# Which head of a quad ScalarE exponentiates in the second attention, and where in its order it does so

## The reference

```python
q = (hidden_states @ wq.T).reshape(B, S, HEADS, HEAD_DIM).transpose(0, 2, 1, 3)   # 32 heads of 8
k = (hidden_states @ wk.T).reshape(B, S, HEADS, HEAD_DIM).transpose(0, 2, 1, 3)
v = (hidden_states @ wv.T).reshape(B, S, HEADS, HEAD_DIM).transpose(0, 2, 1, 3)
scores = jnp.einsum('bhqd,bhkd->bhqk', q, k) / scale
scores = scores + _rel_bias(rel_pos, S)[None, None]
attn = jax.nn.softmax(scores, axis=-1)
ctx = jnp.einsum('bhqk,bhkd->bhqd', attn, v)
return ctx.transpose(0, 2, 1, 3).reshape(B, S, HIDDEN) @ wo.T
```

## Time and profile before

| | us |
|---|---|
| median of 3 runs | 876.03 |
| lowest and highest | 875.99, 877.25 |
| the profiled execution's own time | 876.34 |
| its span on the core | 874.6 |
| second attention in it (first scores to last mix) | 354 to 670 |
| TensorE matmul busy over the span | 806.8 |
| VectorE, ScalarE, GpSimd busy | 667.3, 579.4, 422.2 |

### The profile page before, as it was taken

The page is one execution under the profiler, slowest core; times in us unless marked ns, Lnnn a source line. Parts: engine busy times, 40 slices in busy tenths (PEclk is TensorE's granted clock), DMA queues, the critical chain, the costliest instruction groups (busy, mean ns, idle before and its releaser), DMA issues.

```text
span 874.6 us, 20901 instructions
## 1 busy us (share of the span) xinstructions
PE 806.8 (92%) x7097; PEld 677.9 (78%) x7097; DVE 667.3 (76%) x2136; ACT 579.4 (66%) x1232; POOL 422.2 (48%) x725
## 2 busy tenths in 40 slices
PE   4876999999999999899999999999998999999994
PEld 3554778888888899667777777777766988999984
DVE  5987889888896555778898888979886463487657
ACT  2777868687787533677878777777766233366646
POOL 0353223233253311576767667676765357355423
PEclk9899999999999999999999999999999899999998
DMA  7111220201001010111010211201013112345444
GB/s 218 35 40 43 80 86 12 87 14 37 26 1 49 25 38 25 43 34 31 22 55 23 63 42 37 66 22 43 23 59 120 37 64 95 92 129 134 128 161 170
DMA packets 55017, 54.86 MB, mean 63 GB/s; under 512 B 18209, under 2 KB 49185, under 8 KB 54914
## 3 DMA queue, kind: packets, MB, share of 16 engines
q1 hardware_dynamic: 51506, 44.18, 17.1%
q0 software_dynamic: 3408, 9.34, 3.1%
HBM read 32.85 MB, written 20.65 MB: 61 GB/s over the span
## 4 chain that ended last, share of the span: by engine, by line
PE 68%; DVE 15%; ACT 9%; issue 6%; POOL 1%; DMA 1%; DVEq 0%; ACTq 0%; SPq 0%; POOLq 0%
PE ps L448 13%; PE ps L449 12%; PE ps L450 12%; PE ps L992 10%; PE ps L1003 5%; PE ps L684 3%; PE ps L731 2%; DVE G L2182 2%; PE ps L771 2%; PE ps L976 2%; DVE wu_rows L2182 2%; ACT G L1596 1%; PE ps L1249 1%; PE ps L753 1%; PE ps L1213 1%
## 5 line engine op out<-in xcount | busy, mean ns | idle before, releaser
L2568 POOL TENSOR_SCALAR_AFFINE_SELECT G<-G 128x256 f32<-128x256 f32 x128 | 75.9, 617 | 150.1 <-ACT G L1422 149.9
L1596 ACT ACTIVATE G<-ps 128x512 f32<-128x512 f32 x184 | 102.7, 602 | 39.9 <-PE ps L992 38.3
L448 PE MATMUL ps<-WU 128*128 128x256 f32 x384 | 116.3, 303 | 11.4 <-DVE WU L1977 6.5
L2616 POOL TENSOR_SCALAR G<-G,small 128x256 f32<-128x256 f32 x214 | 99.8, 483 | 51.6 <-DVE small L2182 49.9
L2182 DVE CUSTOM_DVE_ANT_0 G<-ps,nb 128x256 f32<-128x256 f32 x296 | 108.3, 420 | 10.6 <-PE ps L731 9.4
L449 PE MATMUL ps<-WU 128*128 128x256 f32 x384 | 108.3, 282 | 0.0
L450 PE MATMUL ps<-WU 128*128 128x256 f32 x384 | 108.3, 282 | 0.0
L2616 POOL TENSOR_SCALAR wu_rows<-wu_rows,small 128x256 f32<-128x256 f32 x154 | 71.7, 482 | 38.7 <-DVE small L2182 37.7
L448 PEld LDWEIGHTS ps<-WU 128*128 128x128 f32 x384 | 72.8, 190 | 18.0 <-DVE WU L1977 7.3
L992 PE MATMUL ps<-ident,G 128*128 128x128 f32 x592 | 83.5, 278 | 3.0 <-ACT G L1596 2.9
L2182 DVE CUSTOM_DVE_ANT_0 wu_rows<-ps,nb 128x256 f32<-128x256 f32 x216 | 79.5, 420 | 7.4 <-PE ps L731 6.5
(11 more groups left out here) (267 smaller groups left out, 2356.2 us busy)
## 6 DMA issues: line engine op xcount, KB each, us to landing
xs<-G SPq DMA_DIRECT2D x8, 645.0 KB, 6.6
G<-xs SPq DMA_DIRECT2D x39, 128.0 KB
G<-x SPq DMA_DIRECT2D x17, 256.0 KB, 3.1
G<-in_x SPq DMA_DIRECT2D x16, 256.0 KB, 2.8
wu_rows<-yy SPq DMA_DIRECT2D x8, 512.0 KB, 7.0
x<-G SPq DMA_DIRECT2D x15, 256.0 KB, 2.2
wu_rows<-in_wu SPq DMA_DIRECT2D x8, 384.0 KB, 4.9
wraw<-in_wu SPq DMA_DIRECT2D x16, 128.0 KB, 2.2
```

The lines of the kernel that those rows point to most:

```text
L448: pe.matmul(o, lh, rh, start=start, stop=False, skip_group_check=True)
L1596: act.activation(probT(n), halves(2 + n % 2), ACT.Exp).then_inc(probT_taken, 1)
L2568: m = pool.affine_select(out=u, in_=u, compare_op=ALU.is_ge, fill=0.0, base=0, pattern=[[0, 2], [1, P]], channel_multiplier=-1)
L2616: m = pool.tensor_scalar(p, p, -1.0, mneg[:, k:k + 1], ALU.mult, ALU.add)
```

## The change

In the slots with three heads on GpSimd the first head of the quad, and no longer the last, is ScalarE's. Its exponential stands between the two pairs of takes (behind what already stood between them) and no longer at the slot's end. GpSimd shifts heads 1, 2 and 3 of the quad in the place of 0, 1 and 2. Which semaphore a `turn` waits for and whether a `take` is an Exp or a copy follow the head (`on_pool`). Slots 0 and 4 (two heads each) and slot 3 (none on ScalarE) stay.

```diff
         def shifts(n):
             quad, j = divmod(n, 4)
-            return (sum(POOL_SHIFTS) * (quad // QUADS) + sum(POOL_SHIFTS[:quad % QUADS])
-                    + min(j + 1, POOL_SHIFTS[quad % QUADS]))
+            before = sum(POOL_SHIFTS) * (quad // QUADS) + sum(POOL_SHIFTS[:quad % QUADS])
+            return before + sum(on_pool(4 * quad + k) for k in range(j + 1))
+        def on_pool(n):
+            quad, j = divmod(n, 4)
+            few = POOL_SHIFTS[quad % QUADS]
+            return j > 0 if few == 3 else j < few
 # TensorE, turn(n)
-                    if j < POOL_SHIFTS[quad % QUADS]:
+                    if on_pool(n):
                         pe.wait_ge(prob_shifted, shifts(n))
                     else:
                         pe.wait_ge(prob_ready, n + 1 - shifts(n))
 # ScalarE, take(n)
-                    if n % 4 < POOL_SHIFTS[n // 4 % QUADS]:
+                    if on_pool(n):
                         act.activation(probT(n), halves(2 + n % 2), ACT.Exp).then_inc(probT_taken, 1)
 # ScalarE, one(i, first, left)
                         if q == 5 and left:
                             stage_v(2, i + 1)
                         if q == 7 and left:
                             q_heads(2, i + 1, 1)
+                        if POOL_SHIFTS[q] == 3:
+                            exponential(H2 * i + 4 * q)
                         if before >= 0:
                             take(before + 2)
                             take(before + 3)
...
-                        for j in range(POOL_SHIFTS[q], 4):
-                            exponential(H2 * i + 4 * q + j)
+                        if POOL_SHIFTS[q] == 2:
+                            for j in range(2, 4):
+                                exponential(H2 * i + 4 * q + j)
 # GpSimd
-                    for j in range(POOL_SHIFTS[q]):
-                        shifted(H2 * i + 4 * q + j)
+                    for j in range(4):
+                        if on_pool(4 * q + j):
+                            shifted(H2 * i + 4 * q + j)
```

More of the change, by code:

```diff
@@ L979, in turn @@
                 def turn(n):
-                    quad, j = divmod(n, 4)
                     if n == 0:
                         pe.wait_ge(ffn_step, 3 * iterations[1] - 2)
-                    if j < POOL_SHIFTS[quad % QUADS]:
+                    if on_pool(n):
                         pe.wait_ge(prob_shifted, shifts(n))
```

## The result

| | before | changed |
|---|---|---|
| median of 4 runs, us | 876.64 (875.99 to 878.23) | 882.11 (881.51 to 884.63) |
| profiled execution, us | 876.34 | 882.60 |
| its span, us | 874.6 | 880.5 |
| second attention, first scores to the scores of the last slot, us | 306.94 | 311.86 |

The first three of the four runs before are those of the median 876.03 above. The changed kernel takes 1.0065 times as long, with a 95% interval of 1.0047 to 1.0082. By this ratio it is 5.7 us more, by the two medians 5.5; 4.8 (0.55%) had been predicted.

A forecast was written before the change was run, and what follows sets the result against it. The prediction took waits at handovers between engines, not any engine's amount of work, to bound the kernel. Its terms, 3.15 + 2.0 - 0.33 = +4.8 us on the median of 876.03, gave 880.8 us (879.5 to 882; wide 877.6 to 884.0).

The forecast's parts named there:

- What bounds the kernel: Whole kernel: no engine's amount of work is at stake; what counts is which engine waits for another at each handover.
- rival A: Second attention: TensorE is full, so nothing moves; time 876.0 us, chance 0.08.
- Slot 5: Batches 0 to 6: exponential behind `stage_v` delays the take of 18, then the turn of 22; 0.45 a batch, 3.15 in all.
- The steps: Slots 5 and 6: 0.75 from a take's start to the turn it releases, 0.66 from a turn to its take.
- Slots 1 and 2: Late `x_hi` delays VectorE's `x_lo` and the scores of slot 3: 0.36 in batches 2 to 6, 0.2 in batch 1.
- Last batch: No `stage_v` in its slot 5, so the turn of 22 starts earlier: gain of 0.33, once.
- a cover of 0.3: Slot 6: head 23's late take still precedes the mix's second half with 0.3 to spare; without it, up to 0.3 a batch.
- Slots 6 and 7 in the other batches, and GpSimd's later shifts: Takes behind the moved exponentials, and GpSimd shifting the quad's last head instead of its first: all cost nothing.
- The sum: Whole execution: 3.15 + 2.0 - 0.33 = +4.8 us, 0.55%, giving a median of 880.8 us.
- the narrow range: Whole time: the forecast's own range, 879.5 to 882 us, given chance 0.60.
- the wide one: Whole time: 877.6 to 884.0 us, also taking in one loss absorbed (chance 0.18) or covers failing (chance 0.06).
- Rival C: Slot 5's free end pays: the take of 20 is no longer held; 0.36 gained in 8 batches, 873.1 us, chance 0.08.

The follow-up runs named there:

- Slot 5 alone: Kernel before, with only slot 5 as in the change (head 20's exponential behind `stage_v`, ahead of the takes of 18 and 19): ratio 1.0033, second attention +2.64 us.
- the split exponential: Kernel before, with only slot 5's first head on ScalarE, half its exponential ahead of `stage_v`, half behind: ratio 0.9990, second attention -0.16 us.
- the one ahead of `stage_v`: Kernel before, with only slot 5's first head on ScalarE, its whole exponential ahead of `stage_v`: ratio to before 0.9956, second attention -2.78 us.
- slot 1 alone: Kernel before, with only slot 1 as in the change (head 4's exponential ahead of the takes of 2, 3 and `x_hi`): ratio 1.0017, second attention +1.92 us.
- Slots 2, 6 and 7 alone: Kernel before, with only slots 2, 6 and 7 as in the change, slots 1 and 5 as before: ratio 0.9997, second attention +0.31 us.
- the exponential of slot 1 behind `x_hi`: Changed kernel, with head 4's exponential in slot 1 moved behind `x_hi`, to the slot's end: ratio to before 1.0037, second attention +3.94 us.

## Why the prediction was right, and where its sizes were off

**What bounds the kernel** held: with no engine's work changed, the time moved by who waits for whom. The waits of TensorE after the change, from 355 to 676 (as the earlier trace rows: us, times, longest):

```profile
PE ps L997 <- ACT G L1603: 6.8, 12, 0.7
PE ps L737 <- DVE small L2190: 2.9, 4, 1.1
PE ps L1008 <- ACT G L1601: 2.8, 8, 0.7
PE ps L997 <- ACT G L1601: 0.6, 1, 0.6
```

The waits of turns (L997) for takes were 4.2 us and are 7.4, nearly all with a plain copy as releaser (L1603): the turn of 20 now waits for the copy of 18. That is slot 6's share. The waits of mixes for takes (L1008, 2.8 as before) and of scores for VectorE (L737, 2.9 and before 2.8) hardly moved; slot 2's share does not show in this list. Matmul busy time in a batch was 38.55 and is 38.61, while the batch grew from 39.50 to 40.28. So a row nearly full of matmul time did not mean that TensorE couldn't be delayed, and rival A falls. The Trainium skill (Perfetto Trace Analysis, Identifying the Most-Contended Engine) calls that busy time no good measure of how close TensorE is to its limit; this trace agrees.

**Slot 5.** Forecast 0.45 for each of batches 0 to 6, measured 0.41 to 0.43 (2.93 in all, forecast 3.15). The steps were 0.72, 0.66 and 0.73 where I had taken 0.75, 0.66 and 0.75: the turn of 20 waited 0.73 (forecast about 0.8), and that of 22 came 1.39 behind it (forecast less than 1.5). Slot 5 alone, the split exponential and the one ahead of `stage_v` show the mechanism.

**Slots 1 and 2.** Forecast 0.36 in batches 2 to 6 and 0.2 in batch 1, in all 2.0; measured 2.13. VectorE's loss at `x_lo` is 0.74 - 0.39 = 0.35, exactly the forecast one. The mix's second half, 0.25 late where the forecast had it within 0.2, adds 0.04 (slot 1 alone against the whole change); I had called it nearly covered and put it at 0.01. Batch 2 gives only 0.31, batch 1 gives 0.24.

**Last batch.** Forecast a gain of 0.33, measured 0.06. The turn of 22 did come earlier: 1.86 after its slot's scores instead of 2.18 (658.40 less 656.22).

```profile
661.50 0.51 PE L737 MATMUL ps<-RT 32*128 32x256 f32 x8
...
663.36 1.13 PE L997 MATMUL ps<-ident,G 128*128 128x128 f32 x8 [0.33 <-ACT G L1603]
664.42 2.17 PE L1008 MATMUL ps<-G 128*18 128x256 f32 x32
```

But the mix behind it takes 2.17: its second half waits for the take of 23, which stands behind slot 6's exponential. ScalarE's exponential of 24 and takes of 22 and 23, and the weight loads of the mix's second half:

```profile
663.60 0.91 ACT L1590 ACTIVATE G<-G,small 128x256 f32<-128x256 f32 x2
664.40 1.08 ACT L1601 ACTIVATE G<-ps 128x512 f32<-128x512 f32 x2
```

```profile
665.53 0.57 PEld L1008 LDWEIGHTS ps<-G 128*18 128x18 f32 x16 [0.55 <-ACT G L1601]
```

This is the one step that failed. I had given slot 6 a cover of 0.3 for all batches. In the middle ones four transposes stand between the turn of 23 and the mix; the last batch doesn't have them, and the cover with them. Slots 2, 6 and 7 alone, which have that exponential and not slot 5's gain, lose 0.24 there. Slot 5 alone, which has no exponential there, keeps the gain, with a mix of 1.92:

```profile
661.72 1.14 PE L999 MATMUL ps<-ident,G 128*128 128x128 f32 x8 [0.33 <-ACT G L1605]
662.79 1.92 PE L1010 MATMUL ps<-G 128*18 128x256 f32 x32
```

**Slots 6 and 7 in the other batches, and GpSimd's later shifts:** forecast nothing, and slots 2, 6 and 7 alone showed nothing outside slot 2 in batches 0 to 6 (0.01 or less).

**The sum:** +4.8 forecast, +4.92 in the second attention, +5.7 by the ratio of the times (4.1 to 7.2 by its interval). The forecast median was 880.8 and the measured one 882.11: 0.1 above the narrow range (879.5 to 882), inside the wide one. That the second attention comes within 0.1 of the sum is in part luck: 0.22 too much for slot 5 stand against 0.27 too much gain in the last batch and 0.13 too little for slots 1 and 2; the other slots gave 0.08 back. The remaining microsecond of the profiled pair is not in the changed code, and the forecast had no term for it (below).

**Rival C**, the free end of the slot, was not wrong as a mechanism: its 0.36 a batch is what the kernel with the exponential ahead of `stage_v` gained. It decided at the point named, the start of the take of 18.

## What to carry to other kernels

Where two engines hand a small ring of buffers to and fro, as here, a piece of work put ahead of a hand-over delays it from the moment at which the partner would have been ready, and the round trip that follows (turn, take, turn) starts later by as much. It costs even when the engine's own work up to the next item is the same in sum. Put such a piece where the engine idles already: here the right side of one copy of 0.48 us made the difference between +0.42 and -0.36 us per batch. And check the cover of each moved piece in the first and last passes of a loop too, where the neighbours that provide it are missing.

## What the runs showed of the hardware

The profiled executions differ ahead of any changed instruction. Windows from 50 to 100 us of three kernels (columns as in the earlier trace rows), before:

```profile
50.00:100.00 50.00, 38.60 (x334) 30.42 (x334) 40.57 (x66) 38.65 (x67) 18.08 (x28) 0.94 0.18 54
```

changed:

```profile
50.00:100.00 50.00, 38.56 (x320) 30.63 (x321) 38.79 (x65) 36.85 (x64) 16.88 (x27) 0.90 0.18 54
```

and slot 5 with its exponential early:

```profile
50.00:100.00 50.00, 39.30 (x313) 31.00 (x313) 37.73 (x61) 36.06 (x63) 17.60 (x28) 0.85 0.18 53
```

The granted TensorE clock in this window is 0.94, 0.90 and 0.85, in the order of the start of the second attention: 354.36, 0.30 later, 2.22 later. In the traces of all twelve kernels the three with 0.85 or 0.86 start it at 356.47 to 356.68, and eight with 0.90 to 0.95 at 354.24 to 355.06. One more (the exponential of slot 1 behind `x_hi`) has 0.90 too and starts it at 356.21, so the clock of this window doesn't tell it all, and no run tried it as a cause. Through the attention the clock is 1.00 in all twelve.

Whole times scatter by several us: 35 runs of the kernel before, taken beside the first experiments, lie between 875.37 and 881.45, and the profiled execution of the kernel with slot 5 early took 878.38 where its median is 874.89. The slots other than 2 and 6 agree with those of before within 0.03 in every one of the other eleven traces. So effects of 0.3% are read better from the slots than from the whole.
